# Inverting the softmax row sums of three half batches where they stand in PSUM, in an AdaLN transformer block on one NeuronCore

## The reference

```python
mod = (silu(c) @ wmod)                       # six rows per sequence: sa, ca, ga, sb, cb, gb
h = layernorm(x) * (1 + ca) + sa
#   attention block on h, 16 heads of 16 channels, causal, at most 128 tokens back
q, k, v = heads(layer_norm(h, ln1) @ Wq + bq), ...
attn = softmax(q @ k.T / 4 + band_mask)      # exp(...) / row sum
ctx  = attn @ v
h1 = h + ctx @ Wo + bo
h2 = h1 + gelu(layer_norm(h1, ln2) @ W1 + b1) @ W2 + b2
x  = x + ga * h2                             # ga, gb kept at least 0.25 from zero
h = layernorm(x) * (1 + cb) + sb
x = x + gb * (sigmoid(xr @ Wr.T) * (relu(xk @ Wk.T) ** 2 @ Wv.T))   # xr, xk mix a token with the one before it
```

## Time and profile before

| | us |
|---|---|
| median of three runs | 619.79 (619.2 to 621.26) |
| the profiled execution, own time | 619.02 |
| its span in the profile | 617.3 |
| PE busy | 560.3 (91%) |
| PEld busy | 436.6 (71%) |
| ACT busy | 446.9 (72%) |
| DVE busy | 417.1 (68%) |
| POOL busy | 378.1 (61%) |

### The profile page before, as it was taken

One profiled execution on the slowest core, in us unless ns is written; L12 is line 12 of the kernel. 1 busy time (PEld: TensorE's weight loads), 2 busy tenths in 40 slices (PEclk: granted clock), 3 DMA queues, 4 the chain that ended last, 5 costly groups with the idle time before them and its releaser, 6 DMA issues.

```text
span 617.3 us, 16387 instructions
## 1 busy us (share of the span) xinstructions
PE 560.3 (91%) x6448; PEld 436.6 (71%) x6448; DVE 417.1 (68%) x830; ACT 446.9 (72%) x749; POOL 378.1 (61%) x610
## 2 busy tenths in 40 slices
PE   8798987889898998999899989899999999999996
PEld 5467765666766776677667767677777768877785
DVE  4786676794656968786967777757766484465453
ACT  2616676679868787887879686978697798956642
POOL 4277527738947357676776679575748377953330
PEclk9999988989999999999999999999999999999999
DMA  5555435413224034422334152332522134111111
GB/s 163 218 162 129 115 83 161 121 53 81 74 70 111 20 86 123 102 77 71 101 96 116 43 142 88 90 91 74 135 49 69 47 87 122 55 29 36 44 44 34
DMA packets 46363, 55.72 MB, mean 90 GB/s; under 512 B 11643, under 2 KB 33469, under 8 KB 46286
## 3 DMA queue, kind: packets, MB, share of 16 engines
q1 hardware_dynamic: 44454, 53.81, 31.8%
q10 hardware_dynamic: 1832, 0.87, 0.6%
HBM read 22.31 MB, written 4.49 MB: 43 GB/s over the span
## 4 chain that ended last, share of the span: by engine, by line
PE 54%; DVE 20%; ACT 13%; issue 6%; POOL 4%; DMA 2%; ACTq 0%; SPq 0%; DVEq 0%; POOLq 0%
DVE nmax L1853 5%; PE rest L361 4%; PE rest L486 3%; PE quad L398 3%; PE rest L447 3%; PE rest L474 3%; PE rest L498 3%; PE quad L342 3%; PE rest L449 3%; PE rest L448 3%; DVE hid_lo L1914 2%; ACT p L1151 2%; PE quad L307 2%; DVE quad L1850 2%; ACT rest L1202 2%
## 5 line engine op out<-in xcount | busy, mean ns | idle before, releaser
L2588 POOL TENSOR_SCALAR_AFFINE_SELECT p<-p 128x448 f32<-128x448 f32 x64 | 39.0, 610 | 88.1 <-ACT p L1151 63.5
L1853 DVE TENSOR_REDUCE nmax<-quad 128x8 f32<-128x1032 f32 x64 | 78.9, 1233 | 2.2
L430 PE MATMUL rest<-bt_hi,w_hi 128*128 128x256 f16 x256 | 70.2, 274 | 5.0 <-DVE hid_lo L1914 3.5
L1151 ACT ACTIVATE p<-quad,scale_s 128x576 f32<-128x576 f32 (+1 forms) x73 | 59.0, 823 | 20.0 <-PE quad L342 19.7
L1202 ACT ACTIVATE rest<-rest,bias,scale_g 128x256 f32<-128x256 f32 x128 | 62.8, 533 | 12.0 <-PE rest L432 11.5
L447 PE MATMUL rest<-w_hi,hid_hi 128*128 128x256 f16 x256 | 69.9, 273 | 1.7 <-DVE hid_lo L1914 1.7
L432 PE MATMUL rest<-bt_hi,w_lo 128*128 128x256 f16 x256 | 69.8, 273 | 0.0
L431 PE MATMUL rest<-bt_lo,w_hi 128*128 128x256 f16 x256 | 69.8, 273 | 0.0
L449 PE MATMUL rest<-w_hi,hid_lo 128*128 128x256 f16 x256 | 69.8, 272 | 0.0
L448 PE MATMUL rest<-w_lo,hid_hi 128*128 128x256 f16 x256 | 69.8, 272 | 0.0
L1914 DVE SCALAR_TENSOR_TENSOR hid_lo<-rest,inv_f,hid_hi 128x512 f16<-128x512 f32 x64 | 46.5, 740 | 29.1 <-ACT hid_hi L1212 29.1
(11 more groups left out here) (239 smaller groups left out, 1544.4 us busy)
## 6 DMA issues: line engine op xcount, KB each, us to landing
k_st<-k_two SPq DMA_DIRECT2D x64, 128.0 KB, 2.5
v_blk<-vn SPq DMA_DIRECT2D x16, 512.0 KB, 6.0
q_st<-q_two SPq DMA_DIRECT2D x64, 64.0 KB, 2.2
k_st<-k_two SPq DMA_DIRECT2D x64, 64.0 KB, 2.0
rb<-den_rows SPq DMA_DIRECT2D x16, 256.0 KB
x<-x SPq DMA_DIRECT2D x16, 256.0 KB, 3.0
out<-x SPq DMA_DIRECT2D x16, 256.0 KB, 2.2
xa<-x SPq DMA_DIRECT2D x7, 512.0 KB, 4.3
```

Source lines behind the costliest of these rows:

```text
L430: e.matmul(dst, w1_hi[:, k, ms], bt_hi[:, k, :], start=(k == 0), stop=False)
L1151: e.activation(p32[gp % SLOTS][:, c0:c0 + 2 * w].rearrange("p (n c) -> p n c", n=2), (rest if gp < APART else quad)[:, b0 % HQ:b0 % HQ + 2 ...
L1853: e.tensor_reduce(nmax[:, :, :, qt].rearrange("p a j -> p j a"), quad[:, :, 2 * QB - 2:2 * WIN].rearrange("p j (c a) -> p j a c", a=2), AX ...
```

## The change

For `u` = 0, 1 and 15 the detour is dropped. A new step `invert` on DVE takes the reciprocal of the 128x512 row sums as they stand in the bank of `quad` and writes it straight to `rb`; the bank is free when it has finished. `copy_den`, `fold_den`, `divide`, `save_den` and `spread_den` are left for `u` = 2 to 14 (`folded`), with their semaphore counts shifted by two. Three ACT copies (L1137), nine DMAs of SP and three small reciprocals go; three large reciprocals come.

```diff
+    EARLY = 2
+        def folded(u):
+            return EARLY <= u < LAST
             def copy_den(u):
-                if not 0 <= u < NU:
+                if not folded(u):
                     return
                 e.wait_ge(s_av, u + 1)
-                hold(e, s_rc, DMA * u)
+                hold(e, s_rc, DMA * (u - EARLY))
...
+            def invert(u):
+                if not 0 <= u < NU or folded(u):
+                    return
+                e.wait_ge(s_av, u + 1)
+                hold(e, s_ct, u)
+                e.reciprocal(rb[:, :], ring_s.at["den", u][:, :]).then_inc(s_dc, 1)
+
             def scale_c(u):
                 if not 0 <= u < NU:
                     return
-                e.wait_ge(s_rb, DMA * (u + 1))
+                if folded(u):
+                    e.wait_ge(s_rb, DMA * (u + 1 - EARLY))
+                else:
+                    e.wait_ge(s_dc, u + 1)
...
-            warm(0, 8)
             setup_first()
```

More of the change, by code:

```diff
@@ L656, in _ @@
             scores(7, 0, 2)
-            values(1, 1)
+            maxima(2, 3)
+            scores(7, 2, 4)
             max_rows(2)
-            scores(7, 2, 4)
             project(3)
@@ L2177, in _ @@
             setup_w1()
+            low_qk(3)
+            invert(1)
+            scale_c(1)
+            maxima(3, 0)
             setup_f2()
-            low_qk(3)
-            maxima(3, 0)
             low_a(2)
-            divide(1)
             maxima(3, 1)
@@ L2468, in _ @@
             residual_b(12)
-            divide(15)
+            invert(15)
             gated(11)
```

729 lines of the change are left out of this document (356 added, 373 removed).

## The result

| | before | changed kernel |
|---|---|---|
| median of 20 runs each, us | 619.61 | 623.21 |
| range of the runs, us | 617.24 to 622.04 | 620.01 to 626.28 |
| the profiled execution, own time, us | 619.02 | 624.0 |
| its span, us | 617.3 | 622.2 |

The ratio is 1.0057 with an interval of [1.0042, 1.0072]: the change makes the kernel 0.57% slower. The forecast was 615.2 us and faster, with a range that ended at 620.0; it was wrong in sign and range. None of the four rivals was what happened. Medians here are over all executions of a kernel; the ratios leave out the few that took over 1.5% longer than the kernel's fastest.

The account below looks back on a forecast made before the run. PE's own work bounds the middle, and waits on DVE, ACT and banks bound the start. Gains of 5.4 less 0.3 and 0.5 for the clock gave 4.6 us: 614.4 profiled, 615.2 median, range 612.0 to 620.0.

Parts of the forecast that it names:

- four rivals: Reciprocal 5.44 us (7 in 100) or 4.3 to 4.5 (12); middle loses 3.3 us (15); total below 612 (6).
- The price of the reciprocal: On DVE, a 128x512 reciprocal takes 3.27 us, from the slope between 32 columns and one.
- Rivals 1 and 2: DVE's reciprocal takes 5.44 us, total 621.7 (7 in 100); or 4.3 to 4.5 us, total 618.5 (12 in 100).
- (a), the identity matmuls at the start: On PE, dropping warm(0, 8) gains nothing and may lose by the clock; 0.3 us taken as lost.
- (b), the way to `maxima(1, 0)`: PE calls moved out of the way bring maxima(1, 0) at 46.8 in place of 48.70; 1.9 us earlier.
- To `context(0)`: Fewer identity matmuls at scores(4) and an earlier project(2) gain 2.1 us; context(0) at 69.8, running figure 4.0.
- The two reciprocals: invert(0) and invert(1) hold the quad bank in the start; running figure falls from 4.0 to 2.9, costing 1.1 us.
- clock term: PE's clock may halve after gaps at 75 to 80 and 88 to 93, project(3) 5.2 at worst; 0.5 us counted lost.
- `setup_w2` out of the way: On DVE, setup_w2 moves behind maxima(5)'s first part so low_f(0, 1, 2) comes at once; +2.5, running figure 5.4 at 150 us.
- The middle: Single swaps, same work, no identity matmuls; 0 gained, with 1.5 us to either side.
- The end: invert(15) fits DVE's 3.13 us wait ahead of gated(11) to within 0.1 us; gain 0, loss 0.
- The sum: Whole kernel: 5.4 - 0.3 - 0.5 = 4.6 us saved; profiled execution 614.4, median 615.2.

Follow-up runs that it names:

- e3: The changed kernel with setup_wv moved back on VectorE (behind low_a(0)) and on ScalarE (ahead of high_qk(0)); 616.74 us, ratio 0.9965.
- e1: The kernel before in its own order of calls, with the inversion in place of the detour for u = 0, 1 and 15; 628.5 us, ratio 1.0135.
- e8: The kernel before with only divide(15) replaced by invert(15), the detour kept for u = 0 and 1; 619.24 us, ratio 1.0008.
- e10: The kernel before with setup_wv alone moved on VectorE from behind low_a(0) to behind maxima(0, 1); 618.16 us, ratio 0.9992.
- e13: The kernel before with setup_wv alone moved on VectorE to behind maxima(0, 2); 623.58 us, ratio 1.0073.
- e6: e3 with the last calls of VectorE and GpSimd, from about 480 us on, in the order of the kernel before, invert(15) kept; 616.61 us, ratio 0.9972.
- e5: The changed kernel with setup_wv on VectorE moved from behind maxima(0, 1) to behind low_m(0), ScalarE's order as changed; 617.71 us, ratio 0.9973.

## Why the prediction was wrong, step by step

| step of the prediction | forecast | changed | e3 |
|---|---|---|---|
| reciprocal of 128x512 | 3.27 | 3.35 | 3.35 |
| `maxima(1, 0)` | 46.8 | 50.95 | 46.28 |
| `context(0)` | 69.8 | 75.37 | 69.94 |
| `maxima(2, 3)` | 77.9 | 85.29 | 78.43 |
| `max_rows(2)` | 80.1 | 87.59 | 80.87 |
| `project(3)` takes | 2.6 | 5.3 | 4.7 |
| `context(1)` | 82.8 | 93.02 | 85.71 |
| `maxima(3, 0)` | 91.4 | 101.56 | 94.17 |

**The price of the reciprocal** was right, by the slope between two widths of the same operation. Rivals 1 and 2 fall with it. The reading of the Trainium skill's "VectorE: DVE Perf Modes" as eight cycles a column, which gave 4.4 us as an estimate, does not hold here: 3.35 us for 512 columns.

**(a), the identity matmuls at the start**, was right for these two executions: PE got fast at the same place without them (L510 at 6.51 takes 3.75 us, L517 at 10.20 takes 2.30), and `transposes_a(0)` comes at 21.03 where it came at 21.26. The 0.3 us that I took off were 0. (The clock column shows 1.00 in these first 10 us; that PE ran at 1.2 GHz in them is read from the durations alone.) But it rests on one trace. Of the five profiled kernels that have the eight matmuls (the one before, e1, e8, e10, e13), one, e13, ran `setup_first` in 1.95 us; of the eleven without them, none did. What they are worth in the median stays open.

**(b), the way to `maxima(1, 0)`**, is the step that failed. It counts what moved on PE and the cover on ACT, and leaves out that `setup_wv` moved on DVE: the text doesn't name that call at all. It was free as work (0.9 us, where DVE had gaps) and was not free as a place: beside `modulate_x` it took 4.47 us, `maxima(0, 3)` waited 3.81 us, and the figure of +1.9 became -2.25 (50.95 against 48.70). With the call elsewhere the step gives 46.28, half a microsecond better than forecast. The sign that such a pair is slow stood in the trace of the kernel before, in the 21 instructions counted above and, close to this place, on DVE: a TENSOR_TENSOR of one column took 1.27 us beside POOL's second TENSOR_TENSOR (which ran from 39.39 to 41.75).

```profile
40.49 1.27 DVE L2075 TENSOR_TENSOR scale_s<-inv_s 128x1 f32<-128x1 f32 x1
```

**To `context(0)`**: 2.1 us forecast behind `maxima(1, 0)`; with `setup_wv` early it is 3.9 - 2.4 = 1.5.

**The two reciprocals** were placed rightly: in e3 both waits of PE for them are under 0.3 us, and `maxima(2, 3)` and `max_rows(2)` come within 0.8 us of the forecast. What failed here is the size of the **clock term**. I counted 0.5 us for `project(3)`. In e3 it lost 2.1 us, in the changed kernel 2.7 and 1.7 at `context(0)` besides. (`transposes_a(2)` ran at half the clock in both, 1.94 us, but it took 1.94 us in the kernel before too, from 96.83, so this takes nothing from the figure.) The prediction named these stretches, and took a mean over whether the clock falls where the new list left gaps that made it likely. By the mean clocks of the spans (0.983, 0.989 and, before, 0.990) PE was at half for some 21 us in the changed kernel, 14 in e3 and 12 before.

**`setup_w2` out of the way**: forecast +2.5. From `context(2)` to `context(3)` the changed kernel regains 2.6 us (8.8 to 6.2) and e3 as much, while e1 with the old place regains 0.2. The size is right; the step alone wasn't tried.

**The middle**: forecast 0, with 1.5 to either side; it gained 2.1 in the changed kernel (5.8 to 3.7 from `context(5)` on) and 2.2 in e3, more than the 1.5 that I allowed. A whole microsecond of it comes at one place. Before, PE waited here for DVE (the first pass of `down`):

```profile
474.45 0.28 PE L447 MATMUL rest<-w_hi,hid_hi 128*128 128x256 f16 x1 [1.07 <-DVE hid_lo L1914]
```

and the new list has `up(10, 2, 3)` ahead of `maxima(14, 2)`, so that what it waits for is ready. That is read from the lists and the trace, and wasn't tried alone.

**The end**: forecast 0; it lost 1.2. The reciprocal fits its gap, as forecast (e8). The loss is `mix(11)` and `residual_b` beside POOL, the mechanism of `setup_wv` again, and e6 took most of it away.

**The sum.** Forecast 615.2; with the one call moved back 616.7. That these lie within 1.5 us is in part luck. The forecast was 4.6 us ahead of the kernel before at 150 us and held that to the end. e3 is only 1.4 us ahead at `context(3)`, gains 2.8 by `context(15)`, which were forecast as 0, and loses 1.2 at the end: 3.0 in all. The unnamed move made 6.5 us by the medians (7.9 by the spans), or 5.5 where VectorE's call alone is moved (e5): 3.5 us of it are the two instructions themselves (4.47 - 0.96), and of the rest at least 2.3 are the clock, 1.7 at `context(0)` and 0.6 at `project(3)`.
